# Layer zero's expert blocks: their numbers read into registers in two parts of 22 and 21 instead of four of 11, with two shared products and one shared sum moved across a block's edge

## The reference, cut to what matters

```python
router_logits = jax.nn.sigmoid(x @ gate_w + gate_b)              # 16 experts
expert_values, expert_indices = jax.lax.top_k(router_logits, k=2)
expert_values = expert_values / jnp.sum(expert_values, axis=-1, keepdims=True)
hg = jnp.einsum('bsd,edi->bsei', x, experts_wg)                   # d = 256, i = 128
hu = jnp.einsum('bsd,edi->bsei', x, experts_wu)
all_outputs = jnp.einsum('bsei,eid->bsed', jax.nn.silu(hg) * hu, experts_wd)
selected = jnp.take_along_axis(all_outputs, expert_indices[..., None], axis=2)
expert_weighted = jnp.sum(expert_values[..., None] * selected, axis=2)
return x + _mlp(x, shared_wg, shared_wu, shared_wd) + expert_weighted
```

## Time and profile before

| | us |
|---|---|
| median of three runs | 1767.07 |
| lowest and highest of them | 1762.29, 1773.35 |
| the profiled execution | 1773.69 |
| its span, first to last instruction | 1772.0 |

### The profile page before, as it was taken

How to read it: one execution, slowest core, us unless ns; L and a number is a source line. 1 busy time by engine, 2 the same in 40 slices (tenths; PEclk the granted TensorE clock), 3 DMA queues, 4 the chain that set the end, 5 groups by cost and what they waited for, 6 DMA issues and landing times. The chain is left out here.

```text
span 1772.0 us, 36218 instructions
## 1 busy us (share of the span) xinstructions
PE 1637.6 (92%) x12689; PEld 1356.7 (77%) x12689; DVE 1111.6 (63%) x2667; ACT 881.2 (50%) x2541; POOL 553.2 (31%) x848
## 2 busy tenths in 40 slices
PE   5998799999998889799999879999999979999998
PEld 3665677777776577688888757877888779999987
DVE  4776677777777444477776646666666544444464
ACT  2332565565555143255555534444444457666644
POOL 2112323443433244312211121323322257444410
PEclk8999899999998899899999979999999989999999
DMA  8000243333350453100000020000000042223001
GB/s 260 0 0 18 82 151 120 121 119 119 123 174 12 140 184 115 53 12 12 17 7 1 1 89 19 18 19 18 11 18 1 1 143 72 72 103 111 1 1 43
DMA packets 87549, 114.28 MB, mean 64 GB/s; under 512 B 4805, under 2 KB 76697, under 8 KB 87161
## 3 DMA queue, kind: packets, MB, share of 16 engines
q1 hardware_dynamic: 82280, 99.56, 17.6%
q0 software_dynamic: 5136, 12.98, 2.2%
HBM read 64.68 MB, written 47.84 MB: 64 GB/s over the span
## 5 line engine op out<-in xcount | busy, mean ns | idle before, releaser
L1155 ACT ACTIVATE c_probs<-ps,c_negmax 112x375 f32<-112x375 f32 x256 | 143.5, 580 | 3.7 <-DVE c_negmax L1259 3.7
L1360 PEld LDWEIGHTS ps<-const,c_probs 112*125 112x125 f32 x768 | 97.7, 193 | 44.6 <-DVE c_pT L1284 28.1
L1259 DVE TENSOR_REDUCE c_negmax<-ps 112x2 f32<-112x750 f32 x128 | 114.2, 934 | 21.3 <-PE ps L1391 21.3
L1360 PE MATMUL ps<-const,c_probs 112*125 112x112 f32 x768 | 115.6, 288 | 1.8 <-DVE c_pT L1284 1.0
L2198 PE MATMUL ps<-xnT,wide 128*128 128x224 f32 x512 | 112.4, 369 | 5.0 <-ACT e_gate_up L1974 4.5
L1990 ACT ACTIVATE s_probs<-ps,s_negmax 112x112 f32<-112x112 f32 x256 | 86.5, 364 | 36.9 <-DVE s_negmax L2056 36.9
L2198 PEld LDWEIGHTS ps<-xnT,wide 128*128 128x128 f32 x512 | 96.2, 196 | 11.3 <-ACT e_gate_up L1974 6.4
L3136 DVE TENSOR_TENSOR e_hid_low<-xnT,e_hid_high 128x528 fp32r<-128x528 f32 x56 | 41.0, 733 | 82.8 <-ACT e_hid_high L3036 82.8
L1449 PE MATMUL ps<-parts 128*125 128x256 f32 (+1 forms) x480 | 86.5, 316 | 2.3 <-DVE X L1210 2.3
L1143 ACT COPY c_wkv<-ps 125x672 f32<-125x672 f32 x64 | 46.0, 719 | 81.5 <-PE ps L1360 81.5
L2559 ACT ACTIVATE c_probs<-ps,c_negmax 112x375 f32<-112x375 f32 x128 | 71.7, 579 | 14.6 <-DVE c_negmax L2638 14.6
(11 more groups left out here) (504 smaller groups left out, 5152.2 us busy)
## 6 DMA issues: line engine op xcount, KB each, us to landing
expert_rows<-d_zero SPq DMA_DIRECT2D x16, 2240.0 KB
c_ctx_in<-in_ctx SPq DMA_DIRECT2D x32, 375.0 KB
e_x_in<-expert_rows SPq DMA_DIRECT2D x43, 128.0 KB, 2.2
expert_rows<-e_y POOLq DMA_DIRECT2D x43, 128.0 KB, 2.1
e_w_gate_even<-in_L_ffn_w_gate SPq DMA_DIRECT2D x4, 1024.0 KB, 5.2
e_w_fc_even<-in_L_ffn_w_c_fc SPq DMA_DIRECT2D x4, 1024.0 KB, 7.4
e_w_proj_even<-in_L_ffn_w_c_proj SPq DMA_DIRECT2D x4, 1024.0 KB, 10.3
c_kv<-in_L_ffn_w_gate SPq DMA_DIRECT2D x4, 1024.0 KB, 5.0
```

What stands on the lines that cost most here:

```text
L1155: last = nc.scalar.activation(probs[:, g % 2, r, :], ps[:T, r, 0:S], ACT.Exp, bias=negmax[:, par, h:h + 1], accum_out=sums[:, par, h:h + 1])
L1259: nc.vector.tensor_reduce(negmax[:, par, h:h + 3:2], ps[:T, 2 * piece:2 * piece + 2, 0:S], AX.X, ALU.max, negate=True).then_inc(max_done, 1)
L1360: last = nc.tensor.transpose(ps[:KC, bank + r % 2, k * T:(k + 1) * T], probs[:, g % 2, r, k * KC:(k + 1) * KC], ident[:T, :T])
```

## The change

It does four things. `CHUNK` goes from 11 to 22, so each of the three engines reads its numbers with two instructions, of 22 and 21 numbers. Both of TensorE's stand before its loop: one between the two halves of `shared.down`, one behind the turning of blocks 0 and 1. SP's second stands behind its fourth block, POOL's second directly behind its first. Two products of the second half of the shared expert (`up(0)`, first output, two of four) move out of `experts_0` to the end of the stage before, on TensorE. The last shared sum of the stage before, on VectorE, moves to the start of `experts_0`. And TensorE no longer waits for the sums of its own half before the loop; blocks 0 and 1 are turned, and copied by VectorE, ahead of the last of those sums.

```diff
@@ context_attention_0 @@
             shared.add(dve, 0)
             dispatch.choose(dve, B - 1, 1, ("sigmoid", "best", "hot"))
-            shared.add(dve, 1)
...
             shared.down(pe, 0)
             shared.down(pe, 1)
+            for c in range(2):
+                up_product(nc, sh, dispatch.w, B // 2, shared.bank(0, 0), 0, c)
@@ experts_0 @@
-    IN_SLOTS, CHUNK, LATER = 4, 11, 8
+    IN_SLOTS, CHUNK, LATER = 4, 22, 8
...
             for j in range(BLOCKS):
-                if j and j % CHUNK == 0:
-                    at = loaded_values(sp, 1, j, REGIONS * ROWS - TILE)
+                if j == IN_SLOTS:
+                    at += loaded_values(sp, 1, CHUNK, REGIONS * ROWS - TILE)
...
             pool.wait_ge(plan_ready, 1)
+            at = loaded_values(pool, 1, 0, REGIONS * ROWS - TILE) + loaded_values(pool, 1, CHUNK, REGIONS * ROWS - TILE)
             for j in range(BLOCKS):
-                if j % CHUNK == 0:
-                    at = loaded_values(pool, 1, j, REGIONS * ROWS - TILE)
...
+            for n in range(2):
+                add_shared(nc, sh, B // 4 + 2 * n, n).then_inc(late_added, 1)
             dve.wait_ge(gate_mm, 1)
...
+            take_rows(0)
+            take_rows(1)
             shared.add(dve, 1)
...
-            up(0)
+            shared.up(pe, 0, 1)
+            shared.up(pe, 1, 0)
             pe.wait_ge(table_ready, 1)
...
-            up(1)
-            for k in range(2):
-                shared.down(pe, k)
-            pe.wait_ge(shared.hidden_done, 2)
-            pe.wait_ge(shared.added, 4)
+            shared.up(pe, 1, 1)
+            pe.wait_ge(late_added, 2)
+            shared.down(pe, 0)
             pe.wait_ge(plan_ready, 1)
+            experts = loaded_values(pe, 0, 0, E0)
+            shared.down(pe, 1)
...
+            turn_rows(0)
+            turn_rows(1)
+            experts += loaded_values(pe, 0, CHUNK, E0)
...
-                    if j + 3 == len(experts) < BLOCKS:
-                        experts.extend(loaded_values(pe, 0, j + 3, E0))
...
-            experts = list(loaded_values(pe, 0, 0, E0))
```

More of the change, by code:

```diff
@@ L946, in scatter, with add_shared, up_product, __init__ @@
                                          in_=self.rows[:, u, :], in_offset=None).then_inc(self.scattered[u], 16)
+def add_shared(nc, sh, q, n):
+    x = sh.X[:, q:q + 2, :]
+    return nc.vector.tensor_tensor(x, x, sh.ps[:T, 4 + n, :].rearrange("p (j d) -> p j d", j=2), ALU.add)
+def up_product(nc, sh, w, at, bank, n, c):
+    x = sh.xnT[:, c, at:at + SharedExpert.G, :].rearrange("p b t -> p (b t)")
+    return nc.tensor.matmul(bank, w.gate_up[:, E0, c, n * I0:(n + 1) * I0], x, start=(c == 0), stop=(c == 1))
 class SharedExpert:
     G = 4
-    def __init__(self, nc, sh, w, dispatch, sem, start, hidden):
+    def __init__(self, nc, sh, w, dispatch, sem, start, hidden, given=0):
         self.nc, self.sh, self.w, self.dispatch, self.start, self.hidden = nc, sh, w, dispatch, start, hidden
+        self.given = given
         self.up_mm, self.silu_done, self.hidden_done, self.down_mm, self.added = (
@@ L1484, in experts_0 @@
         BANK_X, BANK_GU, BANK_H, BANK_Y, BANK_PLAN = 0, 2, 4, 5, 7
-        shared = SharedExpert(nc, sh, w, dispatch, sem, B // 2, [hid_s[:, k, :] for k in range(2)])
+        shared = SharedExpert(nc, sh, w, dispatch, sem, B // 2, [hid_s[:, k, :] for k in range(2)], given=2)
         gate_mm = sem("gate_mm")
@@ L1502, in loaded_values @@
                 skip_runtime_bounds_check_because="the table is made on the chip from counts that the shapes bound")
-            return values
+            return list(values)
         FIRST_PART, CONTEXT_AT = 10, 28
@@ L1628, in _ @@
             nc.vector.tensor_tensor(sh.kept_weight[:, :, :], sh.kept_weight[:, :, :], bc(total_weight[:, :], 2), ALU.mult)
+            take_rows(0)
+            take_rows(1)
             shared.add(dve, 1)
             def step(j, u):
[L1632 to L1636, removed]
+                if j >= 0 and present(j + 2):
+                    take_rows(j + 2)
                 if present(j):
@@ L1665, in _ @@
         def _(pe):
-            def up(k):
-                for n in range(2):
-                    shared.up(pe, k, n)
             dispatch.gate(pe, B, 0).then_inc(gate_mm, 1)
```

41 lines of the change are left out of this document (23 added, 18 removed).

## The result

| | us |
|---|---|
| before, median of 12 runs | 1766.94 |
| changed, median of 12 runs | 1760.21 (1756.39 to 1765.91) |
| ratio, 95% interval | 0.9964 (0.9947 to 0.9982) |
| span of the profiled execution, before and after | 1772.0, 1759.3 |

A second comparison of the same pair (the last experiment) gave 0.9969 (0.9949 to 0.9989). The change makes the kernel 0.3 to 0.4% faster, about 6 us, where 9.6 us had been forecast; that is inside the 1% that the forecast called no change.

The account below looks back on a forecast made before the run. TensorE was taken to set the pace, 92% of the span, with three register loads interrupting its loop. 10.6 us back in the loop less 1.0 at the head gave 9.6 less: 1767.07 to 1757.5 us, range 1748 to 1766.

Parts of the forecast that it names:

- The three loads in the loop: TensorE's block loop: taking out its three register loads returns 4.8 + 1.96 + 3.87 = 10.6 us, bounds 7.5 and 11.5.
- The edge: Border to the stage: VectorE's last sum moves behind it, TensorE does two more products ahead; the inside starts 0.7 us earlier.
- The products ahead of the table: Head, eight passes: end at 602.85 at half clock, near 599.8 at full clock, where the table decides, 2.3 us better.
- The price of a load: TensorE's head: loads of 22 and 21 numbers cost 3.6 us each, the 22 between 1.5 and 5.9.
- The rivals on the load's price: Numbers paid one by one: 5.9 us per load, time 1761.9, chance 0.2. Mostly fixed price, full clock: 1753.5, chance 0.15.
- The mark for the first load: Sign in the profile after: TensorE's first register load takes 3 to 4.4 us; 5.9 or under 2 would favour rivals.
- TensorE standing still for the first load: Head, between the second layer's halves: load of 3.6 us, TensorE still for about 0.6 less, 3.0 us in the chain.
- Rows "just hidden": Head, before the turning: first blocks' rows land near 610.5, TensorE arrives about then or later, so no wait is charged.
- The loop's start: First block's first-layer product at 615.6 us, 1.0 later than before; bounds 612.5 and 620.0.
- the other half of the second layer: Head, behind the first load: 1.96 us, half as fast again if the clock has fallen; 2.6 in the half-clock chain.
- The sum: Whole kernel: 10.6 us back in the loop less 1.0 at the head, 9.6 us less, 1757.5 us.
- The Trainium skill on the load: About 200 ns per register: the two loads take 4.4 and 4.2 us, leaving a gain of about 8 us.

Follow-up runs that it names:

- e1: Changed kernel with the table of block numbers written ten places further right, so the two loads' start addresses swap roles; one execution, 1755.3 us.
- e7: Changed kernel with loads of 32 and 11 numbers and TensorE's second load ahead of the turning of blocks 0 and 1; ratio 0.9955 to the kernel before.
- e8: Kernel of e7 with the next stage's 4 MB of weights started behind the rows of blocks 3, 4 and 6, later loads from block 12; ratio 0.9949.
- e4: Kernel before with CHUNK raised from 11 to 22 and nothing else, TensorE's second load in its loop; one execution, 1763.3 us.
- e3: Changed kernel with TensorE's second load ahead of the turning of blocks 0 and 1 instead of behind it; ratio 0.9958 to the kernel before.
- e10: Kernel of e7 with the three large later-weight loads behind blocks 8, 10 and 13, small ones and context behind 15 to 18; ratio 0.9948.

## Why the prediction was right or wrong

- **The three loads in the loop: right, a little low.** 10.6 us had been forecast to come back, of at most 11.5. Around block 9 four steps took 13.95 us before and two of them 5.02 us after, 7.45 us over the pace against 1.77: all of 5.68 us came back, not 4.8. With the second's 1.96 and the third's 3.86 that is 11.5 us. The transfer waits did not move in where the load had been; they were 1.6 us before and two of 0.9 us over the pace after.
- **The half clock at the loop's start: missed.** The forecast has no term for it. The first three steps took 6.81 us after and 5.09 before, 1.7 us back: the clock was at 0.52 from 616 to 622 us, where the long pause had just been. So the loop gained 9.7.
- **The edge: right.** 0.7 us forecast, 0.69 measured, and the clock stayed full, in this profile and in every experiment that has the moves. The products ahead of the table ended when the working for a full clock had them, and the table decided.
- **The price of a load: wrong.** "So 22 numbers cost between 1.5 ... and 5.9 us" and "the same 3.6 us" for the load of 21 named the number of values as the only cause. The load of 22 took 2.11 us and the load of 21 took 5.00, where 3.6 had been forecast for each. The rows held the clue: loads of the same 11 numbers at 1.51 and 2.95 us. The working called the difference "whatever made the loads in the loop longer" and left it unnamed. It is the start address, and e1 shows it. The rivals on the load's price, one number each or mostly fixed, were each right for one of the two forms. The mark for the first load, 3 to 4.4 us, was missed as well.
- **TensorE standing still for the first load: wrong.** The forecast charged 3.0 us of standing still for it. The load ran from 602.4 to 604.5 us beside the first half of the second layer (602.81 to about 604.8), whose products were already queued, and the pause was nothing. The forecast's own rows had the overlap, but it allowed for only 0.6 us of it.
- **Rows "just hidden": wrong.** The rows were there when the forecast had them, near 610.5 (TensorE turned them from 610.46). It was TensorE that did not arrive "at about 610.5 or later in either case": with the full clock and no pause for the first load it was done with the shared expert at 606.73, and waited 3.74 us. SP's first transfer stayed at 606.82 although the stage began earlier, because the scatter landed no sooner, SP's wait for it growing from 0.7 to 2.9 us. So the 4.3 us that TensorE gained ahead of that point were lost, and what the long load added came on top. e7 and e8 show both.
- **The loop's start: right by luck, since errors cancelled.** 615.6 forecast, 615.97 measured. For a full clock across the edge, which came true, the working had 614.3. Against its terms the first load gave back 3.0 us, the other half of the second layer 0.6 (1.96 for 2.6) and the turning 0.3; the wait for rows, put at nothing, cost 3.7, and TensorE stood 4.73 us for the second load and not 3.0. Together with 0.2 us at the table that is 1.7 us more.
- **Small slips in its sums.** Two loads of 5.9 us are 4.6 us more than two of 3.6, not 4.4. The lower bound of 7.5 us for the loop is not the sum of its parts (3.0 + 1.96 + 3.87 = 8.8). 1.96 us half as slow again are 2.9, not 2.6. None of them decides anything here.
- **The sum.** 9.6 us forecast, 8.6 in the stage by the trace, 6.7 by the medians. The loop's pauses gave 0.9 more than forecast, the half clock at its start took 1.7, and the head with the edge cost 1.1 (1.8 - 0.7) for a forecast 1.0. What lies between 8.6 and 6.7 is within the interval of the timing and has no cause shown.
- **The Trainium skill on the load.** About 200 ns per register, of the Trainium skill's "Runtime: NRT & Kernel Launch", section "Instruction fetch mechanics", is near the long form (0.23 us per number by e1, 0.26 by e4) and far from the short one (0.05). Here the start address, of which that section says nothing, decides by a factor of over two.

## What to carry to other kernels

When the same instruction with the same operands' size shows two durations in a trace, look for what differs in its operands, the address among them, before averaging them into a forecast. In this kernel loads of several numbers into registers were short where they began at a multiple of 16 bytes of the table, and a table that is read in pieces of 11 or 22 numbers mostly does not; try that first. And where a head of a stage gets faster, ask first which transfer ends it: here a scatter behind 4 MB of weights that nobody wanted yet took back all that TensorE had won, until those weights were cut up and started later.

## What the runs showed of the hardware that I had not expected

- A register load's time depends on its start address. TensorE: 11 numbers 1.35 us (byte 128) or 2.95 us (byte 88); 21 numbers 1.63 us (byte 128) or 5.00 us (byte 88); 22 numbers 2.11 us (byte 0) or 5.50 us (byte 40). SP and POOL show the same (22 and 21 numbers on SP: 1.96 and 4.29 us in the changed kernel, 4.93 and 1.46 in e1).
- The load runs on the sequencer beside products already queued: in e3 it started at 604.7, 1.3 us before the last of them ended (602.07 + 3.92 = 605.99), and hid behind them and the wait for rows.
- A scatter of rows landed 6.2 us after its issue behind 4 MB of weights (e7) and 2.5 us after it without them (e8); a block's rows of 128 KB took 3.4 us before and 2.1 us in e8.
- What a pause of TensorE costs behind it is no fixed amount. The loop's first three steps took 6.81 and 6.49 us in the two profiles of the changed kernel, whose last pauses were 4.73 and 4.50 us; behind a pause of 3.0 us for the first rows they took 4.00 in e7, with the clock at 1.00, and 5.67 in e10, with the clock at 0.62.
